# Moving one of a step's four scan inputs from VectorE to GpSimd in a fused Mamba, attention and expert-mixture layer

## The reference, cut to what matters

```python
xc = silu(conv(x)); dt = softplus(dt_proj(...) + dt_bias)   # 1024 channels
for n in range(16):                                        # 16 states per channel
    dA[t]  = exp(dt[t] * A[n])
    h[t]   = dA[t] * h[t-1] + (dt[t] * xc[t]) * B[t, n]
    y[t]  += h[t] * C[t, n]
y = (y + D * xc) * silu(z);  out = y @ out_proj_w.T
```

## Time and profile before

| | |
|---|---|
| median of 3 runs | 2571.69 us (2564.22 to 2574.04) |
| the profiled execution | 2574.72 us, of which the span of its instructions is 2572.9 us |
| granted TensorE clock over the span | 0.923 of full speed |
| PE / PEld busy | 2259.0 us (88%) / 1293.3 us (50%) |
| DVE busy | 1866.7 us (73%) |
| ACT busy | 1135.4 us (44%) |
| POOL busy | 390.5 us (15%) |
| the first steady block's 16 steps | from 579.00 to 950 us after the span's start, its first use of y at 960.68 us |

### The profile page before, as it was taken

The page is one execution under the profiler, slowest core; times in us unless marked ns, Lnnn a source line. Parts: engine busy times, 40 slices in busy tenths (PEclk is TensorE's granted clock), DMA queues, the critical chain, the costliest instruction groups (busy, mean ns, idle before and its releaser), DMA issues.

```text
span 2572.9 us, 26553 instructions
## 1 busy us (share of the span) xinstructions
PE 2259.0 (88%) x7968; PEld 1293.3 (50%) x7968; DVE 1866.7 (73%) x1870; ACT 1135.4 (44%) x2716; POOL 390.5 (15%) x310
## 2 busy tenths in 40 slices
PE   6756657999999979999999979999999978799997
PEld 2222222445555544445665544445565634688873
DVE  3599995559899986269999986269999973445443
ACT  2633330356566542266555532266555621244430
POOL 0000000001111111001111111001111111566630
PEclk9777788989999989989899989989999989799998
DMA  1201120136767671227777771227677662212110
GB/s 58 83 25 33 31 84 28 45 116 139 159 154 174 162 171 62 84 102 159 152 160 162 168 170 52 89 89 165 147 160 174 156 151 75 101 62 82 61 53 17
DMA packets 89536, 277.43 MB, mean 108 GB/s; under 512 B 10208, under 2 KB 10336, under 8 KB 87424
## 3 DMA queue, kind: packets, MB, share of 16 engines
q0 software_dynamic: 28416, 102.77, 21.4%
q1 hardware_dynamic: 61056, 173.85, 21.4%
HBM read 167.27 MB, written 4.46 MB: 67 GB/s over the span
## 4 chain that ended last, share of the span: by engine, by line
PE 64%; DVE 20%; issue 8%; ACT 3%; DMA 3%; DVEq 0%; POOL 0%; SPq 0%; ACTq 0%; POOLq 0%
PE pq L1310 11%; PE acc L1400 8%; DVE hs L973 7%; PE acc L1257 4%; PE pq L1355 4%; PE pk L1339 4%; PE pq L1302 3%; PE pk L1376 3%; PE pk L1331 3%; PE pq L1357 3%; PE acc L1389 3%; DMA xc<-hs 3%; PE pq L1535 3%; DVE hs L980 2%; DVE hs L964 2%
## 5 line engine op out<-in xcount | busy, mean ns | idle before, releaser
L973 DVE TENSOR_TENSOR_SCAN hs<-dA,hs 128x1024 f32<-128x1024 f32 x256 | 572.2, 2279 | 0.0
L756 ACT ACTIVATE dA<-dt,aneg 128x504 f32<-128x504 f32 x512 | 337.3, 708 | 372.7 <-DVE hs L973 372.4
L609 POOL DMA_DIRECT2D xc<-hs x192 | 167.3, 918 | 1381.9 <-DVE hs L980 1057.1
L1400 PE MATMUL acc<-wb,oT 128*128 128x512 f32 x768 | 364.4, 620 | 3.5 <-ACT oT L745 3.5
L1310 PE MATMUL pq<-qT,wa 128*128 128x512 f32 x768 | 346.0, 604 | 2.9 <-DVE sc L1034 2.9
L964 DVE TENSOR_TENSOR hs<-u,bc 128x1024 f32<-128x1024 f32 x256 | 301.6, 1222 | 7.8 <-ACT xc L849 7.8
L980 DVE TENSOR_TENSOR hs<-hs,bc 128x1024 f32<-128x1024 f32 x256 | 304.7, 1204 | 0.0
L719 ACT ACTIVATE pr<-sc,mx 128x64 f32<-128x64 f32 x512 | 170.8, 335 | 217.6 <-DVE mx L1040 217.6
L1257 PE MATMUL acc<-xnT,wa 128*128 128x512 f32 x512 | 230.6, 604 | 10.6 <-PE acc L1257 4.7
L1310 PEld LDWEIGHTS pq<-qT,wa 128*128 128x128 f32 x768 | 148.8, 195 | 172.0 <-issue 166.4
L1400 PEld LDWEIGHTS acc<-wb,oT 128*128 128x128 f32 x768 | 146.0, 200 | 156.2 <-issue 151.5
(11 more groups left out here) (198 smaller groups left out, 3116.8 us busy)
## 6 DMA issues: line engine op xcount, KB each, us to landing
xc<-hs POOLq DMA_DIRECT2D x192, 512.0 KB, 7.4
bc<-bc_rows SPq DMA_DIRECT2D x64, 512.0 KB, 6.7
wa<-in_wq SPq DMA_DIRECT2D x64, 512.0 KB, 7.5
wb<-in_wo SPq DMA_DIRECT2D x64, 512.0 KB, 4.8
wa<-in_wx SPq DMA_DIRECT2D x16, 512.0 KB, 3.6
wa<-in_wz SPq DMA_DIRECT2D x16, 512.0 KB, 3.7
wb<-in_ow SPq DMA_DIRECT2D x16, 512.0 KB, 5.2
wk<-in_wk SPq DMA_DIRECT2D x32, 256.0 KB, 9.7
```

Of the source, the lines that this page charges most:

```text
L756: ins = S.activation(to[:, :, 1:SEQ], dt[:, s, :].rearrange("p (b t) -> p b t", t=SEQ)[:, :, 1:SEQ], ACT.Exp, scale=aneg[:, s, bass.ds(jj ...
L973: V.tensor_tensor_scan(out=hs[:, c, :], data0=dA[:, c % 2, :], data1=hs[:, c, :], initial=0.0, op0=ALU.mult, op1=ALU.add).then_inc(scd.sem, 1)
L1400: ins = M.matmul(acc[:, t, :], oT[:, h, t * P:(t + 1) * P], wb2(o % 2)[:, h, :], start=False, stop=(stop and h == 1))
```

## The change

In the three steady blocks the input of piece 0, `hs[0] = u[0:2] * B`, is made by GpSimd and no longer by VectorE. The other three stay on VectorE, and so do all four in round 0. GpSimd makes the first of a block after `y0r`. Those of the following steps stand in `sum_y`, behind the wait for `times_c` 2 and ahead of the transfer of piece 2. The semaphore of piece 0 is one of its own (`inp`).

```diff
@@ stages
-        inr = stage("scan_input_ready", NS * NCH)
+        inr = stage("scan_input_ready", NS * (NCH - 1))
+        inp = stage("first_scan_input_ready", NS)
@@ GpSimd
+                def first_input(jj, p):
+
+                    eng.wait_ge(s_bc[p], i * (8 * NS) + jj * 16 + 16)
+                    hold(eng)
+                    G.tensor_tensor(
+                        hs[:, 0, :].rearrange("p (d t) -> p d t", t=T), u[:, 0:2, :],
+                        bc[:, p, 0:1, :].to_broadcast([P, 2, T]), ALU.mult).then_inc(inp.sem, 1)
+
                 def sum_y(jj, p, tail):
 
                     for c in range(NCH):
                         eng.wait_ge(hcd.sem, hcd.upto(i, NCH * p + c) + jj * (2 * NCH))
                         hold(eng)
+                        if c == 2 and not (tail and p == 1):
+                            first_input(jj + p, 1 - p)
                         G.dma_start(xc[:, 2 * c:2 * c + 2, :], hs[:, c, :].rearrange("p (d t) -> p d t", t=T),
                                     accum_op=ALU.add).then_inc(s_y[c], 16)
@@
                     eng.wait_ge(y0r.sem, y0r.upto(i, NCH - 1))
                     hold(eng)
+                    eng.wait_ge(ur.sem, ur.upto(i, 0))
+                    first_input(0, 0)
                     steps(eng, sum_y)
@@ VectorE
-                    bc[:, p, 0:1, :].to_broadcast([P, 2, T]), ALU.mult).then_inc(inr.sem, 1)
+                    bc[:, p, 0:1, :].to_broadcast([P, 2, T]), ALU.mult).then_inc((inp if c == 0 else inr).sem, 1)
@@ scan
-                eng.wait_ge(inr.sem, inr.upto(i, NCH * p + c) + at)
+                if c == 0:
+                    eng.wait_ge(inp.sem, inp.upto(i, p) + jj * 2)
+                else:
+                    eng.wait_ge(inr.sem, inr.upto(i, (NCH - 1) * p + c - 1) + jj * (2 * NCH - 2))
@@ step
-                        scan_input(i, jj, p, 0)
+                        if not attn:
+                            scan_input(i, jj, p, 0)
                         scan_input(i, jj, p, 1)
```

More of the change, by code:

```diff
@@ L542, in _ @@
         def _(eng):
-            lead(eng, ln1r, ln2r, ln3r, wqh, wqs, woh, wos, wkh, wks)
+            lead(eng, inp, ln1r, ln2r, ln3r, wqh, wqs, woh, wos, wkh, wks)
             G = nc.gpsimd
```

## The result

The changed kernel takes 2588.0 us (median of 15 runs, 2578.8 to 2593.7) against 2572.0 (15 runs, 2564.2 to 2581.4). The ratio is 1.0061, 95% interval 1.0049 to 1.0073: 0.6% slower, some 16 us. The profiled execution spans 2586.6 us, 13.7 more than before. Among the executions behind the ratios further down, one of the kernel before took 3901.8 us at a granted clock of 0.55, and it is left out of its ratios.

A forecast was written before the change was run, and what follows sets the result against it. The prediction took TensorE to bound the middle of the blocks, VectorE the first and last steps. Terms of 3 x (1.4 + 0 + 1.2) = 7.8 us on the median 2571.7 gave 2579; full range 2562 to 2606.

The forecast's parts named there:

- TensorE bounds the middle, and the products are worth nothing there.: Mid-block turns: TensorE busy 46.4 of 47.5 us sets the period, so taking products off VectorE gains 0.
- The wait for `kr` would grow to 5 us.: Mid-block turn: VectorE's idle wait for ScalarE's copy `kr` would grow from 2.5 to about 5 us.
- GpSimd's loop has 1.4 us to spare, and the landings shrink when transfers 2 and 3 leave the loads.: Mid-block: GpSimd's loop takes 46.1 of 47.5 us; shorter landings absorb 3.4 of the 4.8 us added, costing 0.
- the 9 to 10 that I had named as the sign: Mid-block: GpSimd's wait for transfers 2 and 3 would shrink from 11.6 to about 9 to 10 us.
- Rival 2: Mid-block: GpSimd's loop becomes the bound; 2592 to 2600 us with half absorbed, 2641 with nothing absorbed; chance 0.27.
- Head +1.4 a block: First step of a block: VectorE's and GpSimd's products run one behind the other, 1.4 us later.
- Tail +1.2 a block: Block end: step 15's product on GpSimd delays step 14's transfers 2 and 3; +1.2 us, ends -3.6 to +2.5.
- steps 13 to 15 run on VectorE's own time: Block end: VectorE sets the pace, so last transfers could start up to 3.6 us sooner.
- Sum: Whole kernel: 3 x (1.4 + 0 + 1.2) = 7.8 us slower, forecast 2579 us.
- the likeliest case's own range: Whole kernel: nothing in the middle, small losses at block ends, 2570 to 2586 us; chance 0.60.
- My rival on the clock: Block ends: shorter VectorE steps restore TensorE's clock, up to 5.5 us a block faster, 2555 us; chance 0.05.
- Rival 3: VectorE's gain comes through at block ends, engines not colliding at the start; -10 us, 2562; chance 0.08.

## Why the prediction was right

- **TensorE bounds the middle, and the products are worth nothing there.** Shown: 42 products moved give 1.0006, all 48 left out 1.0005, and a turn without a low stretch lasts 47.3 us in both. The turn even fell by 0.18 us, which I had not counted. In the chain of waits the value projection L1339 takes 3.76 us before and 3.57 after: `evac_o` no longer gates it, since VectorE's scan and ScalarE's decay come sooner.
- **The wait for `kr` would grow to 5 us.** Wrong in detail. It stayed 2.52. VectorE was held up earlier, at the masked copy and the rotary product, both released by TensorE. The sum, 4.6 us, is what I had expected in one place.
- **GpSimd's loop has 1.4 us to spare, and the landings shrink when transfers 2 and 3 leave the loads.** This was the step I was least sure of. The outcome was right, but the place only in part. The wait behind transfers 2 and 3 is 9.57 and 10.87 us in the turn shown above where it was 12.20 and 11.56, so it gave 3.3 us of the 5.4 that the two products take, and in one of the two steps it stayed above the 9 to 10 that I had named as the sign. The wait behind transfers 0 and 1, which I had left as it was, is 6.53 and 7.33 where it was 7.79 and 8.09 and gave another 2.0. There is more room still: with the product made twice the transfers' part falls from 46.1 to 36.4. Rival 2 is refuted; even 11 us of products a turn leave its period within 0.3 us on average.
- **Head +1.4 a block.** The mechanism, one engine behind the other, is right. The size is 0.8 to 0.9 in blocks 1 and 3, since GpSimd started 0.25 us before VectorE and not 0.1 after, and turning it back gave 1.1 to 1.2.
- **Tail +1.2 a block.** The issue of the last rounds in block 1 is 1.2 and 1.5 later, as worked out, and more than half of the 1.2 comes by the landing that I had followed. The term was still under-sized at 2.4 to 3.0 measured, because I took the last round of 9.65 us as unchanged. It became 10.9 to 12.7. I was wrong, too, that steps 13 to 15 run on VectorE's own time: in step 14 TensorE's scores are the next wait. In blocks 1 and 2 of all profiles with this round (the doubled product apart, where the loads come first), it takes 9.3 to 9.8 us where SP's first load for the next stage comes 2.9 us or more behind its issue (before, step 15 undone, products left out), and 10.6 to 12.3 where it comes 1.1 to 1.8 behind. In block 3, where no `wa` follows, the order is the same by the load of `ctxT`. Before, it came 2.5 us behind the issue at 2098.5 and the round took 9.5, and in the changed kernel 1.3 behind the issue at 2111.7 and the round took 12.7:

```profile
2101.01 1.00 SPq L515 DMA_DIRECT2D ctxT<-in_ctx  x1
...
2113.05 0.33 SPq L516 DMA_DIRECT2D ctxT<-in_ctx  x1
```

  Over the profiles it is 9.5 where the load comes 2.5 us or more behind, and 12.0 to 12.9 where it comes 0.8 to 1.7 behind, the third tail with step 15 undone (0.8) among them. That these loads lengthen the round is argued from this order, since no run moved them alone.
- **Sum.** By stage the measured terms are 3 x 0.85 + 8.1 - 18 x 0.18 = 7.4 us, where the forecast has 7.8. Measured are 16 us. The forecast of 2579 missed by 9 of them, and 2588 lies 2 us above the likeliest case's own range, though inside the full one. What I had put at nothing is the granted clock. In the profiles at hand the changed kernel has one more long turn (3.2 us), and a head 3.4 us longer than its share in block 2, where a low stretch lasts from 1102 to 1124 us that lasted from 1098 to 1114. With these the sum is 14.0, against 13.7 between the two spans. For the average the other executions speak, each with its time and its mean granted clock. Within one kernel 0.001 less of it goes with 1.6 us more (a straight line of one slope through the executions of all kernels, 1.4 to 1.8). The kernel before has 0.9265 on average (63 executions in the later runs), the changed kernel 0.9229, and that makes 5 to 6 us. Compared at the same clock the changed kernel takes 2587.6 us at 0.923 (2 executions) and 2586.8 at 0.924 (3), the kernel before 2577.7 (5) and 2574.9 (7); by the line it is 9.8 us slower (8.3 to 11.4). So of the 16 us some 10 are the kernel's own, where the stages gave 7.4, and the rest goes with the clock. Why the change lowers the clock is not shown. My rival on the clock had the sign wrong. So the verdict holds by its main step, the middle; that the time stayed inside the range is not owed to the sum, which had no term for the clock.
- **Rival 3** (the gain comes through at the block ends) fails. The products left out shorten a clean tail by 0.7 to 1.0 us, since TensorE's scores are the next wait, 1.6 to 2.2 us in step 14.

## What to carry to other kernels

Before moving work off a busy engine, leave it out altogether and time that: here that run came out 0.05% slower, 0.1% faster at best, and with such a ceiling no placement is worth trying. A product moved to a slower engine costs its latency wherever its reader comes next, so look at the first and the last pass of a loop, where no slack covers it. A chain of transfers that waits for landings is worth reading issue by issue: the gain of this study came from one wait that nothing needed.

## What the runs showed of the hardware

- Two engines on SBUF. VectorE's operation of 1.22 us with two SBUF operands lasts 3.18 to 3.37 us when GpSimd's product began 0.06 to 0.25 us earlier, and ends about 1.1 us after it. GpSimd's product lasts 2.35 alone and 3.02 to 3.29 when it begins beside such an operation. Beside the rotary products out of PSUM it stays at 2.35. The Trainium skill, SBUF — State Buffer, "Who interferes with whom", says that a VectorE instruction with two SBUF inputs contends with a GpSimd instruction that reads SBUF, and that whichever issues second is blocked until the other has ended. These rows agree. Other rows of the kernel before, in its last round, agree only in part: beside a one-input multiply of GpSimd a VectorE product with two SBUF operands (L1048) lasts 1.27 us when it begins 0.3 us behind it (2257.94), and 0.69 when it begins 1.8 us behind it, though it ends within it:

```profile
2272.38 2.77 POOL L566 TENSOR_SCALAR wo_hi<-wb 128x1024 fp32r<-128x1024 f32 x1 [6.21 <-PE acc L1389]
...
2274.14 0.69 DVE L1048 TENSOR_TENSOR pr<-pr,sm 128x512 f32<-128x512 f32 x1
```

- An accumulating transfer of 512 KB from SBUF to SBUF lands 10.2 to 12.0 us after its issue in the middle of SP's loads and 4.6 to 6.1 us after it in step 14. Issued behind two products instead of none, the same pair holds GpSimd 7.0 us instead of 11.6.
- The granted clock. The long turns hold one stretch of some 7 us at half clock, the lower of its two levels, 1.2 GHz. In the changed kernel the window around one is

```profile
706.00:713.00 7.00, 7.00 (x25) 4.71 (x25) 7.00 (x7) 3.65 (x10) 1.73 (x2) 0.57 0.42 82
```

  and the turn around it lasts 50.68 us instead of 47.33. TensorE is idle 1.14 us in this turn and 1.14 in the normal one (50.68 - 49.54 and 47.33 - 46.19 in the windows above), so these rows do not say why the clock fell in this one. From one kernel to the next the stretches lie in other turns and tails, and in the changed kernel from one execution to the next as well (6 long turns, then 3), so no run shows that an edit moved them. One is worth nearly four times what the head costs.
